# One branch for TensorE around all rounds, and the two sums of the recurrence swapped between GpSimd and VectorE

## The reference, cut to what matters

```
xk, xv, xr = x * mix + shifted(x) * (1 - mix)          # three mixes
k, v = xk @ Wk.T, xv @ Wv.T ;  sr = sigmoid(xr @ Wr.T)
# per step, with a running maximum for stability:
y  = (e1 * aa + e2 * v) / (e1 * bb + e2)               # numerator / denominator
aa = e1' * aa + e2' * v ;  bb = e1' * bb + e2'
x  = layernorm(x + (sr * y) @ Wo.T)
h  = silu(x @ wg.T / 127) * (x @ wu.T / 127)           # 768 hidden channels
x  = layernorm(x + h @ wd.T / 127)
```

## Time and profile before

| | |
|---|---|
| median of 3 runs | 326.41 us (324.96 to 333.9) |
| profiled execution | 325.1 us, its span 323.3 us |
| mean granted clock of TensorE | 0.954 of 2.4 GHz |
| TensorE busy | 280.9 us (87%) |
| VectorE busy | 272.6 us (84%) |
| ScalarE busy | 218.0 us (67%) |
| GpSimd busy | 148.8 us (46%) |
| DMA | 16.38 MB, mean 51 GB/s |

### The profile page before, as it was taken

One profiled execution on the slowest core, in us unless ns is written; L12 is line 12 of the kernel. 1 busy time (PEld: TensorE's weight loads), 2 busy tenths in 40 slices (PEclk: granted clock), 3 DMA queues, 4 the chain that ended last, 5 costly groups with the idle time before them and its releaser, 6 DMA issues.

```text
span 323.3 us, 4411 instructions
## 1 busy us (share of the span) xinstructions
PE 280.9 (87%) x1250; PEld 205.6 (64%) x1250; DVE 272.6 (84%) x484; ACT 218.0 (67%) x386; POOL 148.8 (46%) x123
## 2 busy tenths in 40 slices
PE   7878869908997999599997999999989998999892
PEld 5624756505885468465885568846785588868782
DVE  4999798629985999669986899899989998989664
ACT  3587767069764688529884498569855986299275
POOL 2564255491569019560378208570759056006030
PEclk9979799976997999989997999999999999999998
DMA  7802200402000301012010401020012001101002
GB/s 256 296 0 65 68 1 2 132 0 65 32 3 3 130 3 65 2 30 102 2 65 5 130 0 65 0 74 23 6 58 65 0 1 67 36 0 65 2 6 99
DMA packets 13531, 16.38 MB, mean 51 GB/s; under 512 B 704, under 2 KB 11200, under 8 KB 13504
## 3 DMA queue, kind: packets, MB, share of 16 engines
q1 hardware_dynamic: 12816, 15.48, 14.5%
q10 hardware_dynamic: 688, 0.53, 0.5%
HBM read 11.81 MB, written 4.19 MB: 50 GB/s over the span
## 4 chain that ended last, share of the span: by engine, by line
DVE 32%; PE 30%; issue 17%; ACT 15%; DMA 3%; DVEq 1%; POOL 1%; SPq 0%; ACTq 0%; POOLq 0%
PE bank_b L980 7%; PE bank_b L1012 6%; PE bank_a L1012 6%; DVE hid L758 4%; DVE wts L633 3%; ACT L512 3%; PE bank_c L970 3%; DVE stats L712 3%; DVE pmax L616 3%; DVE state L662 3%; ACT den L452 2%; ACT x L437 2%; ACT den L458 2%; DVE res L725 2%; DVE rwkv L705 2%
## 5 line engine op out<-in xcount | busy, mean ns | idle before, releaser
L348 POOL TENSOR_TENSOR hlo<-hid,hhi 128x512 fp32r<-128x512 f32 (+1 forms) x36 | 47.5, 1321 | 123.2 <-ACT hhi L496 123.2
L333 POOL TENSOR_TENSOR mix<-mix,xt 128x512 f32<-128x512 f32 x48 | 56.7, 1213 | 13.0 <-ACT mix L422 13.0
L1035 PE MATMUL bank_a<-wd_r,hhi 128*128 128x256 f32 x192 | 47.3, 287 | 4.6 <-DVE hlo L766 4.6
L422 ACT ACTIVATE mix<-dx,par 128x512 f32<-128x512 f32 x48 | 31.2, 710 | 27.0 <-POOL dx L327 26.9
L1035 PE MATMUL bank_a<-wd_r,hlo 128*128 128x256 f32 x192 | 45.6, 279 | 0.0
L980 PE MATMUL bank_b<-woT,rwkv 128*128 128x256 f32 x128 | 34.9, 432 | 8.6 <-issue 7.6
L1035 PEld LDWEIGHTS bank_a<-wd_r,hhi 128*128 128x128 f32 x192 | 36.0, 188 | 7.8 <-issue 7.0
L496 ACT ACTIVATE hhi<-hid 128x512 fp32r<-128x512 f32 (+1 forms) x54 | 31.1, 578 | 10.6 <-DVE hid L758 10.6
L980 PEld LDWEIGHTS bank_b<-woT,rwkv 128*128 128x128 f32 x128 | 27.2, 218 | 14.7 <-issue 8.8
L1035 PEld LDWEIGHTS bank_a<-wd_r,hlo 128*128 128x128 f32 x192 | 36.0, 188 | 0.3 <-issue 0.2
L414 ACT ACTIVATE wts<-wts 128x512 f32<-128x512 f32 (+1 forms) x54 | 27.9, 578 | 8.3 <-DVE wts L633 8.3
(11 more groups left out here) (103 smaller groups left out, 571.7 us busy)
## 6 DMA issues: line engine op xcount, KB each, us to landing
xt<-xT SPq DMA_DIRECT2D x7, 513.0 KB, 4.7
xrow<-x SPq DMA_DIRECT2D x7, 512.0 KB, 3.8
out<-y SPq DMA_DIRECT2D x6, 512.0 KB, 2.8
wg_i<-wg SPq DMA_DIRECT2D x1, 768.0 KB, 7.7
wu_i<-wu SPq DMA_DIRECT2D x1, 768.0 KB, 9.1
wd_i<-wd SPq DMA_DIRECT2D x1, 768.0 KB, 10.4
out<-y SPq DMA_DIRECT2D x3, 256.0 KB, 2.1
xt<-xT SPq DMA_DIRECT2D x2, 257.0 KB, 3.0
```

What stands on the lines that cost most here:

```text
L333: nc.gpsimd.tensor_tensor(mix[:, s, i, h, 0:n], mix[:, s, i, h, 0:n], xt[:, h, 0:n], ALU.add).then_inc(mixed, 1)
L348: nc.gpsimd.tensor_tensor(hlo[:, m, 0:n], hid[:, m % NH, 0:n], hhi[:, m, 0:n].bitcast(f32), ALU.subtract).then_inc(hlo_ready, 1)
L422: nc.scalar.activation(mix[:, s, i, h, 0:n], dx[:, h, 0:n], ACT.Copy, scale=par[:, MIX + i, h:h + 1]).then_inc(dx_scaled, 1)
L1035: mm = nc.tensor.matmul(ffn[:, q, :], hp.bitcast(f32) if full else hp, w[:, m, :], start=(m == 0 and q % 2 == 0 and part is hhi), stop=(m ...
```

## The change

TensorE: the If and Else move from each round's `ffn_products` to the outside of all rounds from 1 on. Rounds 1 to 8 and the last `ffn_products` stand in the code once for the not-wide case and then once more for the wide case, each with a loop of its own.

GpSimd and VectorE: in rounds 1 to 7 GpSimd adds the denominators (den = weight + bb), in two halves, at the start of its round, ahead of all low parts; VectorE adds the numerators (num = kv + aa), 128x1024 at once, between hid 4 and hid 5, in every round. GpSimd's sum waits for the scan of bb of its half and for the `divide` of the round before, VectorE's for `num_new` and the scans of aa. `log_den` waits for both halves. On VectorE `gate_num` comes ahead of both low parts where it stood between them.

```diff
-            def numerator(c, h):
-                pool.wait_ge(aa_ready, c * CH + (h + 1))
-                pool.wait_ge(num_parts, c + 1)
-                n = steps(c)
-                nc.gpsimd.tensor_tensor(num[:, h, 0:n], kv[:, h, 0:n], state[:, 0, h, 0:n],
-                                        ALU.add).then_inc(num_ready, 1)
+            def den_sum(c, h):
+                pool.wait_ge(bb_ready, c * CH + (h + 1))
+                pool.wait_ge(rwkv_ready, c)
+                n = steps(c)
+                nc.gpsimd.tensor_tensor(den[:, h, 0:n], wts[:, OUT, h, 0:n], state[:, 1, h, 0:n],
+                                        ALU.add).then_inc(den_ready, 1)
...
             def round_(j, s, ffn, ahead):
+                if not last(j):
+                    den_sum(j, 0)
+                    den_sum(j, 1)
                 if ffn:
-                    for m in range(NP - 1):
+                    for m in range(NP):
                         low_part(j - 1, m)
-                if not last(j):
-                    numerator(j, 0)
-                if ffn:
-                    low_part(j - 1, NP - 1)
-                if not last(j):
-                    numerator(j, 1)
...
             def log_den(c):
-                sc.wait_ge(den_ready, c + 1)
+                sc.wait_ge(den_ready, c * CH + CH)
...
                 num_new(j)
                 hidden(3)
-                den_sum(j)
+                if first(j) or last(j):
+                    den_sum(j)
                 hidden(4)
-                if first(j) or last(j):
-                    numerator(j)
+                numerator(j)
...
                     hidden(5)
+                    gate_num(j)
                     if ffn:
                         low_part(j - 1, NM - 2)
-                    gate_num(j)
                     if ffn:
                         low_part(j - 1, NM - 1)
                     divide(j)
...
-            def round_(j, s, ffn, nxt):
+            def round_(j, s, ffn, nxt, full=False):
                 if ffn:
-                    with pe.If(any_wide == 0):
-                        ffn_products(j, False)
-                    with pe.Else():
-                        ffn_products(j, True)
+                    ffn_products(j, full)
...
+            def rounds(full):
+                round_(1, 0, True, True, full)
+                round_(2, 1, True, True, full)
+                with pe.Fori(3, NC - 2, 2) as j:
+                    round_(j, 0, True, True, full)
+                    round_(j + 1, 1, True, True, full)
+                round_(NC - 2, 0, True, True, full)
+                round_(NC - 1, 1, True, False, full)
+                ffn_products(NC, full)
+
             with pe.If(any_wide == 0):
-                ffn_products(NC, False)
+                rounds(False)
             with pe.Else():
-                ffn_products(NC, True)
+                rounds(True)
```

More of the change, by code:

```diff
@@ L189, in rwkv_swiglu_kernel @@
         num_parts = sem("num_parts")
-        num_ready = sem("num_ready")
         ln_ready = sem("ln_ready")
@@ L670, in den_sum @@
                 nc.vector.tensor_tensor(den[:, :, 0:n], wts[:, OUT, :, 0:n], state[:, 1, :, 0:n],
-                                        ALU.add).then_inc(den_ready, 1)
+                                        ALU.add).then_inc(den_ready, CH)
             def num_new(c):
@@ L686, in gate_num @@
             def gate_num(c):
[L688 to L693, removed]
+                dve.wait_ge(num_ready_dve, c + 1)
                 dve.wait_ge(recv_ready, c + 1)
```

## The result

The changed kernel takes 310.01 us (median of 4 runs, 309.31 to 310.61); the ratio to the kernel before is 0.952, 95% interval 0.947 to 0.957. On another chip it was 309.28 against 326.42, ratio 0.950 (0.9455 to 0.9545). The forecast was 310.6. The profiled execution took 310.04 with a span of 308.2 us, 15.1 less than the span before, 323.3. The times of before spread from 323.9 to 333.9 over the chips and those of the changed kernel only from 309.0 to 311.5. One disturbed run of each (458.1 and 356.9) is left out of this, and all ratios leave out the slow runs of either kernel, so they aren't the quotients of the medians given.

A forecast was written before the change was run, and what follows sets the result against it. TensorE and VectorE, both above 80% busy, alternate as the limit and the waits between them decide. 325.1 - 9.9 - 1.1 - 3.6 - 1.2 = 309.3 us for the profiled execution, 310.6 against the median; range 308 to 313.

The forecast's parts named there:

- Rounds 2, 3, 4: -9.9: TensorE's gaps before attention_out, from jumping over the other copy of ffn_products, go: -9.9 us together, bounds 0 and -9.9.
- Rival 2: Gaps come from loading new code, in straight code too, or reappear elsewhere; swap alone remains, 321.6; chance 0.11.
- The loop's end: 0: TensorE's jump back at the loop's end stays and shows no gap: 0, bounds 0 to +2.85.
- The 124 matmuls of a round: Count for the changed loop, two rounds, said to just outgrow two instruction blocks under the skill's rule: one stall, 312.2.
- a loader has round 7's code ready when the loop ends: Why straight-code round 7 had no gap: a loader ran ahead during the loop's second pass.
- Round 8: -1.1: TensorE's 1.10 us gap before keep_warm goes and the following chain comes sooner: -1.1, bounds 0 and -1.1.
- the final jump: 0: TensorE's jump past six rounds' code at the end: 6 us of cover over a 2.4 to 2.9 stall, cost 0.
- The swap in rounds 2 to 7: -0.6 each: Without VectorE's wait for GpSimd's numerator, divide comes 0.6 sooner a round, limited by ScalarE's reciprocal; -3.6 in all.
- the early part: GpSimd's denominator adds delay VectorE's scans early in the round: +0.75 and +0.15, VectorE about 1.2 late at hid 2.
- rival 1: Swap's gain eaten at the round's head by scan locks and TensorE standing: 0.15 a round left, 314.5; chance 0.22.
- Round 1: -1.2: Hid 4 comes earlier, divide 1.2 sooner, carried through mixing, xt load and TensorE's 9.73 us wait; bounds 0 and -2.2.

The follow-up runs named there:

- e1: Kernel before with only TensorE's single branch outside the rounds, GpSimd and VectorE as before: 315.25 us against 329.69, ratio 0.961.
- e4: Kernel before with TensorE's loop over rounds 3 to 6 written out, every branch and both copies kept: 331.20 us, one run.
- e2: Kernel before with only the swap of the two sums, TensorE's branches kept in every round: 316.80 us against 329.69, ratio 0.968.
- e3: Kernel before with the If kept in every round but the wide path left out of TensorE's code: 313.99 us, one run.
- e11: Changed kernel with the wide path left out of TensorE's code, so no far jump at the end: 308.15 us, ratio 0.937.
- e6: Changed kernel with the xt load of chunk 3 ahead of the xrow load of chunk 2 on the SP queue: 307.45 us, ratio 0.943.

## Why the prediction was right, and where it wasn't

**Rounds 2, 3, 4: -9.9.** Right in place and cause; the branch alone took 10.8 off these three periods and 9.8 off the span (e1). Rival 2, loading that straight code has too, is out: straight code was loaded as well (10 packets), but no matmul waited for "issue" in e1 or in the changed kernel from 78 to 270 us. What I left unseen is that the price of a gap isn't its own: of 3.3 a gap, about 2.0 was the clock (e4). My periods held it, so the sum was right, but I treated the two parts as separate, and they aren't (e2). Had the swap come first, the branch would have been worth 5.9 (314.1 to 308.2), not 11.

**The loop's end: 0.** Right: no "issue" row between 78 and 270 us. The 124 matmuls of a round in the prediction should be 144, which makes the loop longer, not shorter. Two blocks present and the rest fetched, as the Trainium skill, "Runtime: NRT & Kernel Launch", section "Instruction fetch mechanics", has it, asked for a stall there; no run showed one, and the instruction queue moved nothing in the loop's second pass before. The same section gives TensorE room for 2048 instructions; with that the loop fits, and no stall is due. What it says of a taken branch, a fetch when the target isn't there, is what e3, e4 and the packets show, with gaps of 2.4 to 2.9 us. The prediction's supposition that a loader has round 7's code ready when the loop ends is wrong: it was loaded in round 7 (271.2 us) and covered.

**Round 8: -1.1, and the final jump: 0.** The gap before `keep_warm` went, and the load of ScalarE's last table starts 13.59 behind `attention_out`'s first matmul in place of 14.91, -1.3. The step that failed is "6 us of cover over a stall of 2.4 to 2.9. Cost 0": e11 and the table above show 0.7 us for it in this run, up to 1.5 in others. I had counted only how long TensorE could be late, and from its last matmul to the end there were 6.2 to 6.4 us without a far jump. But the load didn't make the end wait for TensorE; the last store landed later beside it, 2.3 to 3.2 us of waiting in place of 1.7. How long the far load takes isn't measured.

**The swap in rounds 2 to 7: -0.6 each.** -0.69 in the periods (33.64 to 32.95), or -0.75 against e1 (33.70 to 32.95). The mechanism was as laid out: no wait for the numerator, ScalarE's reciprocal late next, `divide` 0.09 behind it. The sizes of the early part were too large: 0.48 and 0.08 for 0.75 and 0.15, and hid 2 is 0.57 later in its round, counted from the round's first gate matmul (217.92 - 209.62 against 230.47 - 222.74 before), not 1.2; no matmul of `gate_up` waits for it. That VectorE's operation with two SBUF inputs and GpSimd's add exclude each other, the rule of the Trainium skill, "SBUF — State Buffer", section "SBUF: two separate sides", the rows bear out within 0.2 us (the ends of GpSimd's rows are rough): the scan from 211.61 lies 0.67 under GpSimd's add (211.19 + 1.09) and lasts 0.48 longer, the one of the earlier trace rows lies 1.13 under it and lasts 0.95 longer. The rule is right that the collisions only move, 1.5 us of them before and after; rival 1 erred in what follows, 0.15 a round, for it set 0.9 of new collisions against the wait removed and left out those that went from low part 4 and the denominators.

**Round 1: -1.2 "which carries through mixing, the load of xt and the wait of 9.73 us".** This step failed. `divide` came 1.1 sooner against the round's first scan (14.09 after it in place of 15.21), but the xt load doesn't follow the mixing: it stands on the SP queue behind the xrow load, and that waits for res1, so for `attention_out`, which starts 16.49 us behind the round's first scan before and after (TensorE no longer waits for `divide` there, but its tiles wait longer for VectorE's late products, up to 1.09 in place of 0.62). The xt load is issued 21.28 behind that scan in place of 21.38, so 0.1 of the 1.1 carries. I followed the chain of semaphores and left out the order of the queue; e6 shows it, 1.8 us.

**What made up for it.** Two misses of 1.8 (start to round 2) and 0.5 (tail) are offset by 1.6 more than forecast in rounds 2 to 7. Of the 1.8, 0.8 is the later start of this trace, which has nothing to do with the change, and 1.2 is round 1's gain that didn't come; round 2 gave 0.2 more than its 0.6 (counted from round 1's first scan, the rows of x1 come at 35.13 for 35.09, round 2's `divide` at 55.68 for 56.49). Of the 1.6 more: 0.4 are the swap's size, and 1.1 is the period from round 2 to round 3, 31.82: it is the first behind the wait of round 1, and in e1 it is 32.65 against 33.70 too. Before, with its gap, it was 36.77 beside 37.23 and 36.86, and I had it as one of three alike. The total was closer than its terms, and that is luck.

## What to carry to other kernels

In these runs a branch over a large piece of code that isn't taken cost what loading the target takes, less the work already queued in front of the jump, and nothing where the code had been run before. Put the copy that runs where its jump has long matmuls ahead of it, or where the jump is short; a single far jump at the end is not free either, if a store is still on its way. And where a load starts later than its semaphores allow, read the queue it stands in: moving one line on the SP queue, and two small pieces of work into idle time ahead of round 1, gave 6.6 us here (309.28 to 302.70), over a third of what the change did.

## What the runs showed of the hardware that I had not expected

- A gap's cost depends on the clock more than on its length: 1.35 and 3.3 us for gaps of 2.44 and 2.77 in one run, 0.7 and 1.05 for 1.84 and 2.15 in another, and the clock fell behind a gap of 2.16 and not behind one of 2.44; what decides stays open.
- A second pass of a loop loads nothing, also where the body holds four copies of 96 matmuls. The straight code right behind it is loaded again, three packets from 271 to 280 us in the kernel before; there this was covered, and with the swap alone 0.79 us of it showed.
- The program's end came 0.7 to 1.5 us later in all seven traces that ended in a far jump of TensorE, and all of it lies in the landing of the last store: 2.3 to 3.2 us of waiting for it in place of 1.7.
